# A graph layer on one core: ranks in the list's pad wait, splits ahead of additions, half of the block loads on ScalarE's queue

## The reference

```python
agg  = segment_sum(x[src], dst, n)
mean = agg / maximum(deg, 1)[:, None]
h    = mean @ W_l + b + x @ W_r
y    = layernorm(x + h * sigmoid(h))
```

## Time and profile before

| | |
|---|---|
| median of 3 runs | 1536.94 us (1535.74 to 1539.15) |
| the profiled execution's own time | 1532.09 us |
| its span | 1530.3 us |
| TensorE, matmuls | 1497.3 us, 98% of the span |
| VectorE | 1320.2 us, 86% |
| ScalarE | 1179.2 us, 77% |
| GpSimd | 1017.3 us, 66% |
| share of the 16 DMA engines taken by the hardware queue that SyncE fills | 70.4% |

### The profile page before, as it was taken

The page is one execution under the profiler, slowest core; times in us unless marked ns, Lnnn a source line. Parts: engine busy times, 40 slices in busy tenths (PEclk is TensorE's granted clock), DMA queues, the critical chain, the costliest instruction groups (busy, mean ns, idle before and its releaser), DMA issues.

```text
span 1530.3 us, 23968 instructions
## 1 busy us (share of the span) xinstructions
PE 1497.3 (98%) x7198; PEld 1239.1 (81%) x7198; DVE 1320.2 (86%) x2090; ACT 1179.2 (77%) x1603; POOL 1017.3 (66%) x1089
## 2 busy tenths in 40 slices
PE   7999999999999999999999999999999999999996
PEld 5877778888888778888888888888888888888885
DVE  7988999999997878888878888888888888888886
ACT  4444333333334799999999999999999999999997
POOL 6446556666662767776757767767677776777783
PEclk9999999999999999999999999999999999999998
DMA  6466689888987799999999999999999999999995
GB/s 205 147 210 204 197 250 262 269 263 267 267 266 229 190 263 290 277 279 280 273 270 294 276 286 270 283 277 271 282 292 273 288 272 281 277 270 281 291 274 196
DMA packets 299350, 397.68 MB, mean 260 GB/s; under 512 B 43037, under 2 KB 145207, under 8 KB 299222
## 3 DMA queue, kind: packets, MB, share of 16 engines
q1 hardware_dynamic: 251239, 321.43, 70.4%
q0 software_dynamic: 46944, 74.22, 17.9%
q10 hardware_dynamic: 1038, 0.50, 0.1%
HBM read 333.87 MB, written 139.67 MB: 309 GB/s over the span
## 4 chain that ended last, share of the span: by engine, by line
PE 83%; DVE 4%; issue 4%; ACT 3%; DMA 3%; POOL 2%; SPq 0%; POOLq 0%; DVEq 0%; ACTq 0%
PE pH L537 75%; PE pT L641 4%; PE pT L610 3%; DMA cor<-correction_rows,node_idx 2%; POOL cor L443 1%; PE pT L548 1%; ACT O L808 1%; ACT cor L755 1%; ACT pH L823 1%; ACT Z L835 1%; DVE Z L914 1%; DVE Z L909 0%; DMA wr_raw<-in_L_gnn_W_r 0%; DMA X<-in_x 0%; DVE w_sum L909 0%
## 5 line engine op out<-in xcount | busy, mean ns | idle before, releaser
L443 POOL DMA_INDIRECT cor<-correction_rows,node_idx x347 | 397.6, 1146 | 246.0 <-ACT cor L755 144.6
L537 PE MATMUL pH<-ws_hi,x_hi 128*128 128x512 f32 x876 | 346.8, 396 | 6.2 <-DVE ws_lo L895 2.2
L537 PE MATMUL pH<-ws_hi,x_lo 128*128 128x512 f32 x876 | 342.7, 391 | 0.0
L537 PE MATMUL pH<-ws_lo,x_hi 128*128 128x512 f32 x876 | 341.7, 390 | 0.0
L537 PE MATMUL pH<-wb_hi,x_hi 128*128 128x512 f32 x688 | 275.6, 401 | 1.3 <-DVE x_lo L1090 1.2
L537 PE MATMUL pH<-wb_hi,x_lo 128*128 128x512 f32 x688 | 268.3, 390 | 0.0
L537 PE MATMUL pH<-wb_lo,x_hi 128*128 128x512 f32 x688 | 267.8, 389 | 0.0
L808 ACT ACTIVATE O<-Z,shift,rstd 128x512 f32<-128x512 f32 x347 | 261.9, 805 | 2.1 <-DVE shift L1137 2.1
L1127 DVE BATCH_NORM_STATS2 stats<-Z 128x6 f32<-128x512 f32 x347 | 219.3, 673 | 0.0
L729 ACT ACTIVATE s_hi<-sums 128x512 fp32r<-128x512 f32 x98 | 62.0, 633 | 196.6 <-DVE sums L1038 196.6
L1119 DVE TENSOR_TENSOR Z<-Z,X 128x1024 f32<-128x1024 f32 x174 | 211.2, 1214 | 1.5 <-ACT Z L835 1.5
(11 more groups left out here) (147 smaller groups left out, 2752.1 us busy)
## 6 DMA issues: line engine op xcount, KB each, us to landing
X<-in_x SPq DMA_DIRECT2D x173, 512.0 KB, 4.6
out<-O SPq DMA_DIRECT2D x173, 512.0 KB, 4.9
xs<-in_x SPq DMA_DIRECT2D x344, 128.0 KB
correction_rows<-c_out SPq DMA_DIRECT2D x98, 256.0 KB, 4.2
light_x<-in_x SPq DMA_DIRECT2D x51, 256.0 KB, 2.9
light_h<-early_product SPq DMA_DIRECT2D x44, 256.0 KB
out<-light_o SPq DMA_DIRECT2D x44, 256.0 KB, 4.2
join_row<-joined SPq DMA_DIRECT2D x98, 64.0 KB, 4.0
```

The source lines that it names most:

```text
L443: g.indirect_dma_start(out=out_, out_offset=None, in_=table, in_offset=bass.IndirectOffsetOnAxis(ap=idx, axis=0), bounds_check=bound, oob_ ...
L537: last = mm(ps, a[:, k], w[:, k], start=(n == 0 and not onto), stop=(n == len(terms) - 1), skip_group_check=onto)
```

## The change

It has three parts. In the list stage, VectorE's loop round 1 moves from behind `dst_found` to ahead of the wait for `dst_padded`. In `node_pair(t)` for t = 1 to 4, VectorE's `split_x(t+1)` moves from behind `moments(t-2)` to ahead of `add_cor(t-1)`. And of the four block loads of every odd pair, the two for partitions 64 to 127 are issued by ScalarE, in its own `load_blocks`, behind `seed(t+1)` and ahead of `reset_cor(t+3)`, with the same wait for `blocks_turned`.

```diff
--- before.py
+++ after.py
@@ -210,6 +210,11 @@
         def turned_by_pe(t):
             return t // 2 + 1 + t // (NP - 1)
 
+        def block_part(t, j):
+            first = BASE + 2 * t * P
+            return (x_raw[32 * j:32 * j + 32].rearrange("r a (i c) -> r (a i) c", i=4),
+                    x[first:first + 2 * P, j * P:(j + 1) * P].rearrange("(i r) c -> r i c", r=32))
+
         def in_blocks(tile):
             return tile[:].rearrange("p k a (i r) -> p (a i) k r", r=32)
 
@@ -337,11 +342,8 @@
 
             def load_blocks(t):
                 wait(sp, blocks_turned, (t + 1) // 2 - 1)
-                first = BASE + 2 * t * P
-                for j in range(4):
-                    sp.dma_start(x_raw[32 * j:32 * j + 32].rearrange("r a (i c) -> r (a i) c", i=4),
-                                 x[first:first + 2 * P, j * P:(j + 1) * P].rearrange("(i r) c -> r i c", r=32)
-                                 ).then_inc(blocks_in, 16)
+                for j in range(2):
+                    sp.dma_start(*block_part(t, j)).then_inc(blocks_in, 16)
 
             def store_out(t, q, u):
                 nt, rows = pair_shape(t)
@@ -799,6 +801,11 @@
                        pT[b][:, 0:nt].rearrange("p a (k r) -> p a k r", k=K)[:, :, :, 0:rows], ACT.Copy
                        ).then_inc(hi_made, 1)
 
+            def load_blocks(t):
+                wait(act, blocks_turned, (t + 1) // 2 - 1)
+                for j in range(2, 4):
+                    act.dma_start(*block_part(t, j)).then_inc(blocks_in, 16)
+
             def normalise(t, q, u):
                 nt, rows = pair_shape(t)
                 b, used = ring(q, u, 2)
@@ -851,6 +858,8 @@
                     light_at(q + 1, reset_light)
 
             single(0, round_x)
+            act.wait_ge(diff_made, ET)
+            load_blocks(1)
 
             def node_pair(t, q, u):
                 if t <= ADDED:
@@ -861,6 +870,8 @@
                     shifted(t, q, u, 1, NP, round_x)
                 if t + 1 >= ADDED:
                     shifted(t, q, u, 1, NP, seed)
+                if by_blocks(t + 3):
+                    load_blocks(t + 3)
                 shifted(t, q, u, 3, NP, reset_cor)
                 lights(light, t)
                 shifted(t, q, u, -3, NP, normalise)
@@ -979,11 +990,11 @@
             found = col[col_bits % 2]
             v.tensor_copy(dst_c, found[:, 0, 0:ET]).then_inc(dst_ready, 1)
             v.tensor_scalar(src_idx[:], found[:, 1, 0:ET], N - 1.0, None, ALU.min)
+            loop_row(1)
             dve.wait_ge(dst_padded, 1)
             v.tensor_scalar(dst_idx[:], dst_c, N - 1.0, None, ALU.min)
             then(v.tensor_copy(dst_f[:, 1:1 + ET], dst_c))
             dve.sem_inc(dst_found, 1)
-            loop_row(1)
 
             dve.wait_ge(consts, 5)
             dve.wait_ge(t_ready, 1)
@@ -1176,9 +1187,11 @@
 
             def node_pair(t, q, u):
                 if 1 <= t <= ADDED:
+                    single(t + 1, split_x)
                     single(t - 1, add_cor)
                 shifted(t, q, u, -2, NP, moments)
-                shifted(t, q, u, 1, NP, split_x)
+                if not 1 <= t <= ADDED:
+                    shifted(t, q, u, 1, NP, split_x)
                 shifted(t, q, u, -1, NP, residual)
                 shifted(t, q, u, -2, NP, make_shift)
                 lights(light, t)
```

## The result

| | before | after |
|---|---|---|
| median of the runs | 1536.44 us (13 runs) | 1540.03 us (13 runs) |
| lowest, highest | 1531.46, 1539.42 | 1536.66, 1542.78 |
| profiled execution, span | 1530.3 us | 1539.8 us |
| mean granted clock | 0.996 | 0.994 |

The two were run again side by side on one chip, which is why the median of before is not the 1536.94 of above. The ratio is 1.0025, with a 95% interval of 1.0016 to 1.0034: **3.8 us slower (2.5 to 5.2)**. The forecast was +2.1 us and a range that ends at +8.

A forecast was written before the change was run, and what follows sets the result against it. TensorE was taken as the bound, its matmuls busy 1497.3 of 1530.3 us. The three parts, 0 + 2.1 + 0, on the median 1536.94 gave 1539.0 us, range 1534 to 1545, called no change that can be told.

The forecast's parts named there:

- when pair 5 is at its late end: Forecast's branch above 0.2% slower: pair 5 starts at its late end and some of what follows slips too; chance 0.09.
- Part 1, 0: List stage: the moved round fits VectorE's 6.78 us pad wait, but the turned list still comes at 122.14; 0 us.
- Pair 2, gain 0.64: Node pair 2: the split moves into VectorE's idle time before the correction lands, removing TensorE's wait; gain 0.64 us.
- Pair 3, gain 0.2: Node pair 3: addition follows ScalarE's rounding and the split; TensorE starts at 507.7 against 507.89, gain 0.2 us.
- the walk: Row-by-row reckoning of pairs 2 to 5 with profiled durations; gave splits ahead of additions +1.0 to +3.1 us, taken +2.1.
- Pair 4, 1.65 later: Node pair 4: its seed hangs on the delayed addition through silu; TensorE starts at 516.1 against 514.45, 1.65 us later.
- Pair 5, 2.1 to 3.1 later: Node pair 5: its seed hangs on a late addition; start 2.1 to 3.1 us later, lower end taken as nearer.
- A third of the later 1.1 comes back: TensorE's later 1.1 us seed wait shrinks when everything before is late; 0 to 1.1 us back, about a third taken.
- Part 3, 0: Two block loads on ScalarE: issues hide under 1.78 us of queued work plus 0.42 us idle per double pair; 0 us.
- The rival of the clock: TensorE's clock falls in the new gaps before pairs 4 and 5, adding 1 to 2 us each: 1541 to 1543; chance 0.15.
- ScalarE as the bound: Every odd pair, seed to bias copy: issues hold ScalarE back, +34 to +42 us, 1571 to 1581; chance 0.10.
- The gains stay: Waits of 0.64, 0.83, 1.22 and later 1.1 us all go, without losses: 3.8 us faster, 1533.1; chance 0.15.

The follow-up runs named there:

- repeated: The whole changed kernel timed a second time against the kernel before: 1.0022 (1536.32 against 1532.91 us).
- part 2 alone: The kernel before with only the splits ahead of additions for t = 1 to 4, timed twice: 1.0014 and 1.0019.
- the first split only: The kernel before with the split ahead of the addition in t = 1 only: 0.9993; the changed kernel with only that split ahead: 0.9995.
- the split ahead of the moments: The kernel before with split first in t = 1, and addition, split, moments in t = 2 to 4: 1.0006.
- three and four: The changed kernel, splits back in the old order, with three or all four block loads of odd pairs on ScalarE: 1.0079 and 1.0310.

## Why the prediction was right where it was, and wrong where it wasn't

The direction and the cause were right: the only part that moves the time is part 2, its losses at pairs 4 and 5 are larger than its gain at pair 2, and the time lies within the range. The size was short, 2.1 us against 3.8 (2.5 to 5.2) and, repeated, 3.4, and with it fell the verdict "no change that can be told": most chance stood there, and the result lies just past 0.2%, with an interval that begins at 0.16%. What came is the branch to which the prediction gave 0.09, "when pair 5 is at its late end".

- **Part 1, 0: right.** Alone it measures 0.9999, and the edge tiles' start moved by 0.1 us. The wait at `dst_idx` is 3.31 in the profiled execution, for the slow copy and a pad that came 0.6 earlier (117.48 + 0.18), but 4.65 to 5.27 in five of the six others, around the 4.8 written; the one at the turned list is 3.43, as written.
- **Pair 2, gain 0.64: right** (0.60 to 0.80 in the four traces).
- **Pair 3, gain 0.2: between.** 0.3 earlier in one trace, level in two, 0.6 later in the profiled one, where the transposes ahead of it waited 0.56 for a load of `X`, which the walk had left out, and the addition came at 512.12.
- **Pair 4, 1.65 later, 8.4 us behind pair 3: right in kind.** It is 8.55 behind pair 3, after 2.84 for the seed. The walk's 2.95 us of busy ScalarE between `silu(1)` and `round_x(4)` came out as 516.33 - 513.37 = 2.96.
- **Pair 5, 2.1 to 3.1 later, the lower end taken as nearer: this is the term that was mis-sized.** The reason given for the lower end, that the gathers which kept GpSimd from 1/sigma would be over, failed: VectorE waited 0.94 us for `rstd` all the same, and again in each of the other traces of part 2 (0.93 or 0.94). From `add_cor(2)` to the block transpose it took 524.31 - 518.67 = 5.64 us, which is the walk's value with that wait (6.76 - 1.1 = 5.66). Then everything went by the upper end, 9.2 us from pair 4 to pair 5, where the walk allowed 8.3 to 9.3. That is +3.3 from pair 3 to pair 5 in place of the 2.3 to 3.3 of the walk.
- **A third of the later 1.1 comes back: wrong for the whole change.** The wait before pair 10 was 1.56 and 1.53 against 1.13. It came back only where pair 6 was late by the clock as well (0.59 and none). That share took what holds the seed as fixed, and it isn't: the seed waits for a gather of GpSimd, and this starts 54.08 us after pair 0 before, and 58.56, 57.99, 57.92 and 57.58 in the four traces with all of part 2, so it moves by 3.5 to 4.5 us with the additions, about as much as the pairs themselves; only in the two traces of part 2 alone is pair 6 later than that (4.8 and 4.3 us), which is where the wait shrinks. With two loads on ScalarE the way from pair 6 to pair 10 is 25.4 to 25.6 us in four traces; before, with the first split only, and with part 1 only it is 24.8 to 25.0 (but 26.7 with the split ahead of the moments, where part 3 is absent too). That would be 0.6 us for part 3, but by pair 24 it is gone again (147.58 against 148.00), and no timed run shows it.
- **Part 3, 0: right, with its reason.** The cover of 1.78 us and the idle 0.42 bound it from above. Two issues took at most 1.70 us in the changed kernel between 700 and 1400 us, within the cover; three and four are past it and cost time, though the count gives their size only roughly.
- **The rival of the clock (0.15, 1541 to 1543): the fall came, its price mostly not.** The gaps were 2.84 and 2.63 us, as worked out, and the clock went to 0.50 behind one of them in three of four traces, never behind both. But the price of one fall, 1.4 us, was hidden under pair 5's wait in one, and partly absorbed at pair 10 in two. The rival forgot what the text itself asks of each stall: what is late next.
- **ScalarE as the bound (0.10): wrong at two issues, right at three and four.** At four the time was 49.5 us over, above the 34 to 42 that the rival had for two. SyncE's and ScalarE's issues of block loads can overlap in time (two of SyncE's from 1012.56 to 1014.20, two of ScalarE's from 1013.19 to 1014.57), so neither waited until the other's two were out. The median of such an issue on ScalarE is 0.42 us in the changed kernel, where SyncE issues two as well, and 0.55 in the kernel with four, where ScalarE issues all; on SyncE it is 0.56 in the changed kernel and 0.49 before. Of the descriptor generator the Trainium skill ("Perfetto Trace Analysis", "DMA Instruction — HWDGE") says that the issuing engines share it and an issue first waits to lock it; these rows show no price of that on ScalarE, and 0.07 us an issue on SyncE in the median.
- **The gains stay (0.15): wrong.** The first split, which alone has nothing to lose, is worth at most 1.8 per thousand by its interval, and shows as 0.7 and 0.5 of one.

## What to carry to other kernels

Before an instruction is put ahead of another on an in-order engine, look up what it waits for and who hangs on what it is put ahead of. Here a split that waits for ScalarE stood before an addition on which, over `silu`, the seed of a later pair hung; putting only the first one ahead, where nothing is behind it, loses nothing. Here issues on a computing engine's queue were free only as long as the work already handed over to that engine lasted, so count: cover plus idle time per round, against the time of the issues in the median and not in the shortest row. And where a range of a term hangs on whether a wait returns, take the end that the existing row shows (0.93 us here) unless a row shows the resource free.

## What the runs showed of the hardware that was not expected

- Gaps on TensorE of 2.6 to 3.2 us between pairs were followed by the lower clock in five of six traces that have them (3 to 4 us of records at or near 0.50, 1.3 to 1.7 us lost), once in each; gaps of up to 1.94 us in the pairs never were. The sixth has two such gaps, 2.83 and 2.62, and no fall, so the length of the gap alone doesn't settle it. What does is open.
- The same predicated copy of 516 columns takes 0.77 to 0.79 us in five of the seven traces with part 1 and 1.90 and 1.77 in two. In the two slow ones a subtraction of GpSimd had begun just ahead of it (112.54 against the copy's 112.56, and 111.77 against 111.92), and the copy ended 0.6 us after GpSimd's end. In two others the copy began first (112.19 and 112.04, GpSimd at 112.38 and 112.40); there the copy took 0.77 and 0.78 and it was GpSimd's 1.3 us that became 1.69 and 1.52. In the other three they did not meet, and both were short. So in these four meetings the one that began second was held back. No run was made for it.
- One execution differs from the next by 1 to 2 us within the first ten pairs. Part 1 alone, worth 0.9999, has its pair 2 after a wait of 1.43 us in place of 0.64, and its pair 24 at 149.71, with a wait of 1.52 us for a load of `X` at 587.19 on the way. So single traces were read here for chains and repeated distances, and the timed ratios for sizes.
